# A fused group-norm and attention kernel: row maxima behind the projection in every unit 0 modulo 4, with shifts, gating and GpSimd's side work at other places

## The chip, the cores and the metric

The kernel runs on one core of a Trainium2 chip. The metric is the device time of one execution in microseconds (us); the median of three runs stands for a kernel.

## The reference, cut to what matters

```python
xn = silu(group_norm(x, gn_scale, gn_offset))          # x: (16, 32, 32, 512), 32 groups
q, k, v = split(einsum('bxyc,cd->bxyd', xn, w_qkv))    # 8 heads of 64
sim = einsum('bhdi,bhdj->bhij', q * 64 ** -0.5, k)     # 1024 x 1024 for each head
out = einsum('bhij,bhdj->bhid', softmax(sim), v)
return einsum('bxyd,dc->bxyc', out, w_out) + b_out + x
```

There are 16 images of 1024 tokens and 512 channels.

## The kernel before, in words

Every engine runs its own list of instructions, written out by hand, and meets the others at semaphores. An image is four **steps** of 16 **units**; a step is one pair of heads, and unit v = 16*s + u of an image is written (s, u) here. Images 2 to 14 repeat one pattern; a loop covers two images, and its back edge lies in front of (2, 0).

Numbers are carried as a high and a low float16 part. In unit v TensorE computes, in this order:

- **scores** of unit v (L1292, L1293): four matmuls of 512 columns into a slot of `ST`. `ST` has two slots, used in turn, so every user of a slot waits until the user before the last has been read (`wait_ring`).
- in even units the **maxima** of a later pair (L1192): four matmuls on 64 rows, into `TP` and into the next slot of `ST`. `maxima_place` says where they stand: 0 is directly behind the scores, 1 behind the product with V, 2 behind the projection. Before the change only the even unit behind a turned output block ((0, 4), (2, 4), (2, 12), (3, 8)) has 2, and u = 2 has 1.
- the **product with V** of unit v - 2 (L1322), into `PV`. The first of each four needs `pv_out`, that is, the sums of the four before have been taken out of `PV`.
- half of a **projection** into `SD` (L1177; a qk, v or out job lasts two units, part 0 in the even and part 1 in the odd one). Part 0 waits until the job before it has been drained (`side_drained`).
- in some odd units a **turn** (transposes): `xt` of the next image's input (L1250, at (0, 1), (0, 5), (0, 7), (0, 9)) or `ot` of an output (L1257, at (0, 3), (2, 3), (2, 11), (3, 7)). It stands in front of part 1 of the projection, or behind it where `turn_late` says so, which is only (0, 3) before.

ScalarE takes two exponentials of each slot, `P32` in float32 (L733) and `Ph` in float16 (L736), then its halves of the drains (L690, L695), the copies of turns (L705, L710) and the next image's `z` and `tanh` (L717, L724), at places in the tables `Z_AT` and `TANH_AT`.

VectorE makes the low probabilities `Pl` = P32 - Ph of one half of the columns (`low_probs`, L960) and GpSimd those of the other half (L615). VectorE's order in unit v is: the sums where v % 4 == 2 (L968 to L970), the drain of the job before (L848, L853, L860), `low_probs` of v - 1, the low part of a turned output (L881), a gating `z <- th, z` where `GATE_AT` says so (L946), then the two row maxima: `top_second` of the `ST` slot (L910; in the even unit, or in the odd one where maxima stand at place 2) and `top_use` of `TP` (L903, odd unit). After the fourth and the eighth block of rows (u = 9 and u = 1) a **shift** `ms <- mx` (L916) follows. SyncE's queue then copies the eight columns out and back as rows: `place_shift` waits for the shift, issues `shift_rows <- ms` (L456), waits for its landing, and issues two `QK <- shift_rows` (L460). Scores of u = 4 need those of u = 1's shift, scores of the next step's u = 0 those of u = 9's. SyncE's queue is in order: at (0, 1), `load_x` stands in front of `place_shift` and waits for the turn of that unit (`xt_filled`), since `x_in` is a single buffer.

GpSimd does in order, in each unit: `low_probs` of v - 1, `normalise` where v % 4 == 3 (L625), the statistics' small work ((1, 2), (1, 5)), `high_xn` (L598) in the unit of a gating and `low_xn` (L592) one unit later, and `add_bias` of the output blocks (L603) at `BIAS_AT` and `LATE_BIAS_AT`.

Of the kernel before, what the change touches and what calls it, by code (L numbers as in the profile page):

```python
# [10 lines left out]
ALU = mybir.AluOpType  # L11
# [119 lines left out]
def turn_late(step, u):  # L131

    return (step, u) == (0, 3)
# [7 lines left out]
def maxima_place(step, u):  # L141


    return 2 if output_turned(step, u) else 1 if u == 2 else 0
# [91 lines left out]
def conv_attention(nc, x, gamma, beta, w_qkv, w_out, b_out, out):  # L236
# [4 lines left out]
    with ctx:  # L241
# [26 lines left out]
        cns = sb("cns", [P, 4], F32)  # L268
# [98 lines left out]
        shift_ready = sem("shift_ready")  # L367
# [28 lines left out]
        def _(sp):  # L396
# [72 lines left out]
            def step(b, s, cnt, first=False, last=False):  # L469
                for u in range(16):  # L470
# [21 lines left out]
                    for pair, qb in unit_shift(s, u, last):  # L492
                        place_shift(b, pair, qb // 4)
# [40 lines left out]
        def _(pool):  # L534
# [95 lines left out]
            def step(b, s, par, first=False, last=False):  # L630
                for u in range(16):
# [48 lines left out]
        def _(act):  # L680
# [136 lines left out]
        def _(dve):  # L817
# [94 lines left out]
            def shift(qb, cnt):  # L912
# [4 lines left out]
                                        ALU.subtract, ALU.mult).then_inc(shift_ready, 1)  # L917
# [54 lines left out]

            def step(b, s, par, cnt, first=False, last=False):
                turned = []
                for u in range(16):
# [22 lines left out]
                    if u % 2 == output_turned(s, u - u % 2):  # L998
                        for use, slot in seconds:
                            top_second(use, cnt, slot)  # L1000
                    for use in unit_max(s, u - 1, last) if u > 0 else []:
                        top_use(use, b + 1, cnt)
                    for _, qb in unit_shift(s, u, last):
                        shift(qb, cnt)
# [458 lines left out]
```

## Time and profile before

| | before |
|---|---|
| median of 3 runs | 3598.46 us (3598.12 to 3598.59) |
| the profiled execution's own time | 3602.31 us |
| its span in the profile | 3600.6 us |
| TensorE matmuls busy | 3453.8 us (96%) |
| VectorE busy | 3047.2 us (85%) |
| ScalarE busy | 2698.3 us (75%) |
| GpSimd busy | 2020.2 us (56%) |
| granted TensorE clock | 0.994 of full speed |

A row of busy time by stretch has the bounds of the stretch and its length in us, then the busy us (and instructions) of TensorE's matmuls, its weight loads, VectorE, ScalarE and GpSimd, the granted TensorE clock as a share of full speed, the busy share of the DMA engines and GB/s. The stretches here begin and end at the first score matmul of a unit.

The span runs from the first to the last instruction. TensorE is nearly always busy, so the length of a unit, from one unit's first score matmul to the next unit's, is the natural measure: all 1024 of them together, with a prologue and an end, make the span. The ends of matmuls are modelled, so starts are the better number. A line of the timeline gives the start and the duration of an instruction (or of several merged ones), both in us, and in brackets how long the engine sat idle before it and for whom.

### The profile page before, as it was taken

To read this page: it belongs to the slowest core of one execution; us is meant where nothing else is said; L and a number is where in the kernel's file an instruction comes from. 1 tells how busy PE (TensorE), PEld (TensorE's weight loads), DVE (VectorE), ACT (ScalarE), POOL (GpSimd) and SP (SyncE) were. 2 spreads that over 40 slices of the span, in tenths; PEclk is the share of its full clock that TensorE was granted. 3 is DMA by queue.
4 is the path that set the end of the run, shared out by engine and by line. 5 is a ranking of instruction groups with operands and counts; after the bars stand their busy time and mean duration, and the time that the engine had idled before them with its cause. 6 is when DMAs were issued, how large, how long until landed. Compare 5 with 4: busy or idle time off the path is not lost. (4 is left out here: it accounts for less than half of the span.)

```text
span 3600.6 us, 89829 instructions
## 1 busy us (share of the span) xinstructions
PE 3453.8 (96%) x31822; PEld 1890.8 (53%) x31822; DVE 3047.2 (85%) x4011; ACT 2698.3 (75%) x2820; POOL 2020.2 (56%) x1998
## 2 busy tenths in 40 slices
PE   6899999999999999999999999999999999999998
PEld 2455555555555555555555555555555555555554
DVE  8788888888888887988888888888888888888887
ACT  3787777878778787787877778777777877877776
POOL 1464655646465474655646556465564656546556
PEclk8999999999999999999999999999999999999999
DMA  2213213222132322223133131321322213232231
GB/s 98 70 37 99 64 35 101 53 82 66 36 100 53 85 63 63 73 60 96 44 76 81 38 99 44 98 65 36 100 53 82 66 41 94 53 86 62 50 88 43
DMA packets 180060, 245.79 MB, mean 68 GB/s; under 512 B 51488, under 2 KB 84256, under 8 KB 179616
## 3 DMA queue, kind: packets, MB, share of 16 engines
q1 hardware_dynamic: 179616, 239.94, 25.6%
q8 instruction: 271, 4.44, 0.6%
q14 instruction: 173, 1.42, 0.1%
HBM read 88.35 MB, written 33.82 MB: 34 GB/s over the span
## 5 line engine op out<-in xcount | busy, mean ns | idle before, releaser
L615 POOL TENSOR_TENSOR Pl<-P,Ph 128x512 f16<-128x512 f32 x1024 | 1284.1, 1255 | 1402.0 <-ACT Ph L736 1394.5
L733 ACT ACTIVATE P<-ST,cns 128x1024 f32<-128x1024 f32 x1024 | 1140.5, 1114 | 818.2 <-PE ST L1293 782.7
L736 ACT ACTIVATE Ph<-ST,cns 128x1024 f16<-128x1024 f32 x1024 | 1133.1, 1107 | 0.3 <-issue 0.3
L960 DVE TENSOR_TENSOR Pl<-P,Ph 128x512 f16<-128x512 f32 x1024 | 1013.7, 990 | 72.8 <-ACT Ph L736 67.9
L1322 PEld LDWEIGHTS PV<-V,Ph 128*128 128x128 f16 x10240 | 760.5, 97 | 295.2 <-issue 127.2
L1322 PE MATMUL PV<-V,Ph 128*128 128x129 f16 (+2 forms) x10240 | 864.0, 210 | 37.8 <-DVE pv_sum L970 28.5
L1322 PE MATMUL PV<-V,Pl 128*128 128x65 f16 x8192 | 832.7, 192 | 1.9 <-issue 1.9
L1292 PE MATMUL ST<-QK 128*128 128x512 f16 x2048 | 777.9, 380 | 36.4 <-DMA QK<-shift_rows 22.2
L1293 PE MATMUL ST<-QK 128*128 128x512 f16 x2048 | 777.0, 379 | 0.0
L1322 PEld LDWEIGHTS PV<-V,Pl 128*128 128x128 f16 x8192 | 721.9, 98 | 66.4 <-issue 0.3
L1177 PE MATMUL SD<-X,wq 128*128 128x512 f16 x3036 | 741.9, 381 | 12.6 <-DVE wq L1067 9.2
L910 DVE TENSOR_REDUCE mx<-ST 128x1 f32<-128x1024 f32 x512 | 622.8, 1216 | 25.9 <-PE ST L1192 25.6
L903 DVE TENSOR_REDUCE mx<-TP 128x1 f32<-128x1024 f32 x512 | 620.7, 1212 | 0.0
L1177 PEld LDWEIGHTS SD<-X,wq 128*128 128x128 f16 x3036 | 278.8, 98 | 334.5 <-issue 28.0
L1177 PE MATMUL SD<-wq,X 128*128 128x512 f16 x1488 | 360.9, 379 | 4.3 <-DVE wq L1067 2.8
L1177 PE MATMUL SD<-wo,OT 128*128 128x512 f16 x1440 | 349.9, 379 | 1.6 <-DVE res L860 1.6
L1192 PE MATMUL TP<-QK 64*128 64x512 f16 x1024 | 317.0, 390 | 20.2 <-DVE mx L903 10.1
L1292 PEld LDWEIGHTS ST<-QK 128*128 128x128 f16 x2048 | 201.2, 98 | 248.5 <-ACT Ph L736 43.3
L848 DVE SCALAR_TENSOR_TENSOR QK<-SD,sc,QK 128x512 f16<-128x512 f32 x253 | 189.5, 749 | 153.7 <-ACT QK L690 133.6
L1192 PE MATMUL ST<-QK 64*128 64x512 f16 x1024 | 317.4, 390 | 0.0
L1293 PEld LDWEIGHTS ST<-QK 128*128 128x128 f16 x2048 | 199.8, 98 | 171.2 <-issue 1.1
L625 POOL TENSOR_TENSOR O<-pv_sum,den 128x256 f32<-128x256 f32 x256 | 224.1, 876 | 1.5 <-DVE pv_sum L970 1.5
(133 smaller groups left out, 2752.3 us busy)
## 6 DMA issues: line engine op xcount, KB each, us to landing
QK<-QK SPq DMA_DIRECT2D x384, 256.0 KB, 4.7
x_in<-in_x SPq DMA_DIRECT2D x61, 512.0 KB, 4.2
res<-in_x SPq DMA_DIRECT2D x120, 256.0 KB, 3.6
out<-res SPq DMA_DIRECT2D x120, 256.0 KB, 2.8
V<-V SPq DMA_DIRECT2D x16, 1040.0 KB, 6.9
QK<-shift_rows SPq DMA_DIRECT2D x256, 64.0 KB, 2.9
V<-in_L_conv_w_qkv SPq DMA_DIRECT2D x4, 768.0 KB, 9.8
shift_rows<-ms SPq DMA_DIRECT2D x128, 2.0 KB, 3.1
```

The lines of the kernel that those rows point to most:

```text
L615: nc.gpsimd.tensor_tensor(Pl[:, v % 4, HALF:], P32[:, v % 2, HALF:], Ph[:, v % 4, HALF:], ALU.subtract).then_inc(lo_pool, 1)
L625: nc.gpsimd.tensor_tensor(O32[:, pair % 2, 4 * q:4 * q + 4, rows_of(hh)], pv_sum[:, half % 2], den[:, half % 2, :].unsqueeze(2).to_broadca ...
L733: nc.scalar.activation(P32[:, v % 2, :], ST[:, slot, :], ACT.Exp, scale=cns[:, 0:1])
L736: nc.scalar.activation(Ph[:, v % 4, :], ST[:, slot, :], ACT.Exp, scale=cns[:, 0:1]).then_inc(exp_done, 1)
L903: nc.vector.reduce_max(mx[:, 0, qb:qb + 1], TP[:], AX.X).then_inc(top_drained, 1)
L910: nc.vector.reduce_max(mx[:, 1, qb:qb + 1], ST[:, slot], AX.X).then_inc(top_read, 1)
L960: nc.vector.tensor_tensor(Pl[:, v % 4, 0:HALF], P32[:, v % 2, 0:HALF], Ph[:, v % 4, 0:HALF], ALU.subtract).then_inc(lo_dve, 1)
L1177: ins = nc.tensor.matmul(bank, stationary(i, c), moving(j, c), start=(c == 0 and i + j == 0), stop=(c == CC - 1 and i == 1))
L1192: ins = nc.tensor.matmul(bank[:, bass.ts(kh, HALF)], QK[r, q_hi, block], QK[r, k_hi, bass.ts(kh, HALF)], start=True, stop=True)
L1292: nc.tensor.matmul(dst, QK1[:, at, 1, kb], QK1[:, at, 0, bass.ts(q, HALF)], start=True, stop=False)
L1293: ins = nc.tensor.matmul(dst, QK2[:, at, 1, kb], QK2[:, at, 0, bass.ts(q, HALF)], start=False, stop=True)
L1322: ins = nc.tensor.matmul(PV[:, cols], stationary, moving, start=kb == qb == n == 0, stop=kb == TB - 1, skip_group_check=True)
```

## The change

- Maxima stand at place 2, behind part 0 of the projection, in every unit 0 modulo 4; u = 2 keeps place 1 and the other even units place 0.
- Turns in units 1 modulo 4 ((0, 1), (0, 5), (0, 9)) stand behind part 1 of the projection.
- VectorE reads both maxima of a unit 0 modulo 4 in the unit behind it; in u = 1 it does so, with the shift, in front of `low_probs`.
- The shift of the first half moves from VectorE at u = 9 to ScalarE at u = 10 (an activation with a scale and a bias column), and its `place_shift` to u = 11. The one semaphore for shifts becomes two.
- `Z_AT`, `TANH_AT`, `GATE_AT`, `BIAS_AT` and `LATE_BIAS_AT` get other units.
- GpSimd waits for VectorE's `low_probs` of v - 1 before a low half or a bias.

```diff
 def turn_late(step, u):
-    return (step, u) == (0, 3)
+    return u % 4 == 1 or (step, u) == (0, 3)
...
 def maxima_place(step, u):
-    return 2 if output_turned(step, u) else 1 if u == 2 else 0
+    return 2 if u % 4 == 0 else 1 if u == 2 else 0
...
-Z_AT = [(1, 7), (1, 8), (1, 10), (1, 14), (2, 2), (2, 4), (2, 8), (2, 10)]
-TANH_AT = [(1, 8), (1, 10), (1, 12), (2, 0), (2, 4), (2, 6), (2, 8), (2, 12)]
-GATE_AT = [(1, 9), (1, 11), (1, 13), (2, 1), (2, 5), (2, 7), (2, 9), (2, 13)]
-BIAS_AT = {(3, 0): 0, (3, 2): 1, (3, 5): 2, (3, 6): 3}
-LATE_BIAS_AT = {(1, 0): 4, (1, 7): 5, (1, 8): 6, (1, 10): 7}
+Z_AT = [(1, 8), (1, 10), (1, 12), (1, 14), (2, 2), (2, 4), (2, 8), (2, 10)]
+TANH_AT = [(1, 9), (1, 11), (1, 12), (2, 0), (2, 2), (2, 6), (2, 8), (2, 10)]
+GATE_AT = [(1, 11), (1, 13), (1, 15), (2, 1), (2, 3), (2, 7), (2, 9), (2, 11)]
+BIAS_AT = {(3, 4): 0, (3, 6): 1, (3, 10): 2, (3, 12): 3}
+LATE_BIAS_AT = {(1, 0): 4, (1, 4): 5, (1, 8): 6, (1, 10): 7}
...
 # SyncE
                     for pair, qb in unit_shift(s, u, last):
-                        place_shift(b, pair, qb // 4)
+                        if qb == 7:
+                            place_shift(b, pair, 1)
+                    for pair, qb in unit_shift(s, u - 2, last):
+                        if qb == 3:
+                            place_shift(b, pair, 0)
...
 # GpSimd
+                    high, low = halves_at(s, u)
+                    if (low and not last) or ((s, u) in BIAS_AT and not last) or ((s, u) in LATE_BIAS_AT and not first):
+                        pool.wait_ge(lo_dve, UNITS * b + v)
...
 # ScalarE
+            def shift(tops):
+                blocks = slice(0, 4)
+                act.wait_ge(top_drained, tops)
+                nc.scalar.activation(ms[:, :, blocks], mx[:, :, blocks], ACT.Identity, scale=-1.0 / (HD * ROWC),
+                                     bias=cns[:, 4:5]).then_inc(shift_ready[0], 1)
...
                     exponentials(b, v, cnt)
+                    if u == 10 and unit_shift(s, u - 1, last):
+                        shift(cnt.top)
...
 # VectorE
+            def maxima(b, s, u, cnt, seconds, last):
+                if u % 2 == (maxima_place(s, u - u % 2) == 2):
+                    for use, slot in seconds:
+                        top_second(use, cnt, slot)
+                for use in unit_max(s, u - 1, last) if u > 0 else []:
+                    top_use(use, b + 1, cnt)
+                for _, qb in unit_shift(s, u, last):
+                    if qb == 7:
+                        shift(qb, cnt)
...
+                    if u == 1:
+                        maxima(b, s, u, cnt, seconds, last)
                     if not (first and v == 0):
                         low_probs(b, v - 1)
...
+                    if u != 1:
+                        maxima(b, s, u, cnt, seconds, last)
```

## Rows read from the trace of the kernel before

**Rows 1.** Busy time by stretch: thirteen images, a plain pair of units, other units
```profile
527.17:3389.75 2862.58, 2791.53 (x25850) 1531.12 (x25848) 2436.87 (x3185) 2186.99 (x2289) 1641.19 (x1638) 1.00 0.27 68
1664.38:1670.77 6.39, 6.39 (x66) 3.43 (x63) 6.13 (x11) 4.25 (x5) 2.92 (x3) 1.00 0.39 103
1641.79:1645.31 3.52, 3.52 (x38) 1.74 (x35) 2.79 (x4) 3.05 (x4) 0.94 (x2) 1.00 0.00 0
1638.05:1641.79 3.74, 3.74 (x37) 2.58 (x36) 2.37 (x3) 2.67 (x4) 2.19 (x3) 1.00 0.15 35
```

**Rows 2.** Waits over the whole run: engine, line, releaser, total us, times, longest
```profile
PE ST L1292 <- DMA QK<-shift_rows: 22.2, 28, 3.0
```

**Rows 3.** Busy time by stretch: unit (0, 5) of image 7
```profile
1645.31:1649.82 4.51, 3.97 (x38) 2.52 (x37) 2.65 (x3) 3.03 (x3) 2.56 (x2) 1.00 0.10 27
```

**Rows 4.** Busy time, then timelines of VectorE and TensorE: (1, 10), image 7
```profile
1716.36:1721.30 4.94, 3.65 (x37) 1.75 (x35) 4.90 (x7) 4.06 (x5) 4.91 (x5) 1.00 0.04 2
...
1714.81 1.51 DVE L946 SCALAR_TENSOR_TENSOR z<-th,z 128x512 f32<-128x512 f32 x1
1717.48 1.09 DVE L916 TENSOR_SCALAR ms<-mx,cns 128x8 f16<-128x8 f32 x1
...
1719.29 0.23 PE L1322 MATMUL PV<-V,Ph 128*128 128x129 f16 x1 [1.16 <-DVE pv_sum L970]
```

**Rows 5.** Busy time by stretch: (1, 8) and (1, 12), image 7
```profile
1709.75:1713.49 3.74, 3.72 (x37) 1.77 (x35) 2.11 (x3) 3.74 (x5) 3.74 (x4) 1.00 0.13 48
1724.17:1727.94 3.77, 3.58 (x37) 1.74 (x35) 3.77 (x5) 3.02 (x4) 3.67 (x3) 1.00 0.41 146
```

**Rows 6.** Busy time by stretch: (2, 2) with (2, 3), images 7 and 8
```profile
1743.60:1753.24 9.64, 7.59 (x74) 4.48 (x72) 6.96 (x11) 7.10 (x9) 5.52 (x6) 1.00 0.31 75
1965.34:1973.74 8.40, 7.59 (x74) 4.48 (x72) 6.88 (x11) 6.87 (x9) 5.29 (x6) 1.00 0.25 39
```

**Rows 7.** Busy time of (2, 5) with (2, 6), and VectorE's timeline there
```profile
1756.75:1763.70 6.95, 6.71 (x62) 3.51 (x61) 6.24 (x10) 6.51 (x8) 5.25 (x5) 1.00 0.70 174
...
1757.85 0.85 DVE L946 SCALAR_TENSOR_TENSOR z<-th,z 128x512 f32<-128x512 f32 x1 [0.71 <-ACT th L724]
1758.63 1.21 DVE L910 TENSOR_REDUCE mx<-ST 128x1 f32<-128x1024 f32 x1
```

**Rows 8.** Busy time by stretch: unit (3, 7) of image 7
```profile
1818.38:1822.32 3.94, 3.94 (x37) 2.51 (x36) 3.14 (x3) 2.62 (x3) 2.14 (x3) 1.00 0.01 4
```

**Rows 9.** Timelines of VectorE and GpSimd: low probabilities beside a bias, (1, 10)
```profile
1719.81 1.64 DVE L960 TENSOR_TENSOR Pl<-P,Ph 128x512 f16<-128x512 f32 x1
...
1719.62 1.29 POOL L603 TENSOR_TENSOR res<-res,bias 128x512 f32<-128x512 f32 x1
```

**Rows 10.** Timelines: a drain in (0, 0), VectorE's maxima in (0, 5), TensorE in (0, 4)
```profile
1627.91 0.75 DVE L848 SCALAR_TENSOR_TENSOR QK<-SD,sc,QK 128x512 f16<-128x512 f32 x1 [1.23 <-ACT QK L690]
...
1645.61 1.22 DVE L910 TENSOR_REDUCE mx<-ST 128x1 f32<-128x1024 f32 x1
...
1643.36 1.46 PE L1177 MATMUL SD<-wo,OT 128*128 128x512 f16 x6
1646.89 1.09 PE L1250 MATMUL ST<-ident,x_in 128*128 128x128 f32 x8 [0.54 <-DVE mx L910]
```

**Rows 11.** Timelines of TensorE and SyncE's queue in (0, 1) to (0, 3)
```profile
1631.37 1.04 PE L1250 MATMUL ST<-ident,x_in 128*128 128x128 f32 x8
1640.21 1.04 PE L1257 MATMUL ST<-ident,O 128*128 128x128 f32 x8
...
1632.58 0.38 SPq L414 DMA_DIRECT2D x_in<-in_x  x1
1633.11 0.37 SPq L456 DMA_DIRECT2D shift_rows<-ms  x1
1637.92 1.10 SPq L460 DMA_DIRECT2D QK<-shift_rows  x2
```

**Rows 12.** DMA issues of the page: count, KB each, median us to landing
```profile
QK<-shift_rows SPq DMA_DIRECT2D x256, 64.0 KB, 2.9
```

More of the change, by code:

```diff
@@ L267, in conv_attention @@
         tot = sb("tot", [P, 8], F32)
-        cns = sb("cns", [P, 4], F32)
+        cns = sb("cns", [P, 5], F32)
         absg = sb("absg", [P, CC], F32)
@@ L366, in conv_attention @@
         v_moved = sem("v_moved")
-        shift_ready = sem("shift_ready")
+        shift_ready = [sem(f"shift_ready{half}") for half in range(2)]
         shift_row = [sem(f"shift_row{half}") for half in range(2)]
@@ L452, in place_shift @@
             def place_shift(b, pair, half):
-                sp.wait_ge(shift_ready, 8 * b + 2 * pair + half + 1)
+                sp.wait_ge(shift_ready[half], 4 * b + pair + 1)
                 sp.dma_start(rows[half].rearrange("h (p j) -> p h j", j=4), ms[:, :, 4 * half:4 * half + 4]
@@ L641, in step @@
                         coefficients(b + 1)
+                    high, low = halves_at(s, u)
+                    if (low and not last) or ((s, u) in BIAS_AT and not last) or ((s, u) in LATE_BIAS_AT and not first):
+                        pool.wait_ge(lo_dve, UNITS * b + v)
                     if not last:
-                        high, low = halves_at(s, u)
                         for i in high:
@@ L916, in shift @@
                 nc.vector.tensor_scalar(ms[:, :, blocks], mx[:, :, blocks], cns[:, 3:4], -1.0 / (HD * ROWC),
-                                        ALU.subtract, ALU.mult).then_inc(shift_ready, 1)
+                                        ALU.subtract, ALU.mult).then_inc(shift_ready[qb // 4], 1)
             def guess(image, tops):
@@ L997, in step @@
                         seconds = [(use, cnt.next_slot()) for use in unit_max(s, u, last)]
[L998 to L1004, printed above, removed]
+                    if u != 1:
+                        maxima(b, s, u, cnt, seconds, last)
                     turned = [(use, cnt.next_slot()) for use in unit_turn(s, u, first, last)]
@@ L1105, in _ @@
             then(nc.vector.reciprocal(cns[:, 2:3], cns[:, 0:1]))
-            nc.vector.tensor_scalar(cns[:, 3:4], cns[:, 2:3], SHIFT_UP, None, ALU.mult).then_inc(setup_done, 1)
+            then(nc.vector.tensor_scalar(cns[:, 3:4], cns[:, 2:3], SHIFT_UP, None, ALU.mult))
+            nc.vector.tensor_scalar(cns[:, 4:5], cns[:, 3:4], 1.0 / (HD * ROWC), None, ALU.mult).then_inc(setup_done, 1)
             dve.wait_ge(setup_done, 1)
```

## The prediction

> **What bounds the kernel.** I first read busy time by stretch. Images 2 to 14 take 2862.58 us, 220.2 us each, TensorE is busy in 2791.5 us of it, and its clock is granted in full throughout [rows 1]. So TensorE's list sets the time, and the question is only where it stands still. I then took the units one by one. A plain pair (even with maxima, odd without) is 6.39 us, an even unit with its maxima at place 2 is 3.52 us, the same as with place 0 in that pair (6.39 less an odd unit of 2.87), and an odd unit with a turn is 3.74 us [rows 1], so a turn costs 0.88. An image without any wait is 32 x 6.39 + 8 x 0.88 + about 0.4 for the two statistics = 211.9 us. The whole prize is therefore some 8.3 us an image, 3.8%. The change removes no work from TensorE and adds none; it can only open or close such gaps. Last I read in which units the gaps lie and which instruction ended them. A unit longer than its plain length is a stall in it or in front of the next scores. All terms below are per image, and 15 images have them (the last has no next image to prepare, the first is nearly regular).
>
> **Gains.**
>
> 1. (0, 5) takes 4.51 us [rows 3] instead of 3.74. The turn starts at 1646.89 after 0.54 us idle, behind the read of the `ST` slot that began at 1645.61 and took 1.22 [rows 10]. Behind part 1 of the projection the turn comes 1.3 us later (1640.21 in a unit starting at 1638.05, against 1631.37 in one starting at 1630.51 [rows 1, 11]), when the read is over. Gain 0.77.
> 2. (1, 10) takes 4.94 us against 3.52: the product with V waited 1.16 us for the sums, which stood behind a gating of 1.51 us and a shift of 1.09 us [rows 4]. The gating leaves (1, 9) and this shift leaves VectorE. In its place both maxima are read in (1, 9), and the sums end about 1.5 us into (1, 10), as the product wants them. Gain 1.4.
> 3. (1, 8) and (1, 12) are 0.22 and 0.25 us too long [rows 5]: a bias behind the Newton steps, and a late read of `TP`. The bias moves to (1, 4), and there pushes the Newton steps, so that ScalarE's exponentials of unit 7 come later and the scores behind (1, 8) wait some 0.1. Gain 0.3.
> 4. (2, 2) with (2, 3) takes 9.64 us in image 7 and 8.40 in image 8, against 3.52 + 3.74 = 7.26 [rows 6]. In the first a shift is held on VectorE just as the 1.09 us one was [rows 4] and then arrives late. Afterwards it isn't held, since it runs before GpSimd has anything to do, but low probabilities and a gating now stand between the shift and the sums of (2, 2). These are two float32 passes of about 0.6 to 0.7 us; the sums end 1.73 us into (2, 2) and not 1.04, the product starts at 1.79, and the pair comes to 8.2 us. Gain between 0.2 and 1.4; I take 0.4, near image 8, because the DMA is waited for in only 28 steps of 64 [rows 2].
> 5. (2, 5) with (2, 6) takes 6.95 us against 6.39: with place 2 in the unit before, gating (1757.85, 0.85 us) and then the read of `ST` (1758.63, 1.21 us) end at 1759.84, and the scores of the next unit start at 1759.89 [rows 7]. (2, 13) with (2, 14) has the same pattern. Both gatings move to 3 modulo 4. Gain 2 x 0.57 = 1.15.
> 6. Turns at (3, 7) (3.94 us against 3.74 [rows 8]) and (2, 11) (half as much) wait for a read pushed by GpSimd's work, which now starts later. Gain 0.3.
> 7. In steps 1 and 3 the shift of u = 1 comes about 0.2 us earlier, because it no longer waits for low probabilities; where the scores of u = 4 wait for its rows that is gained. 0.15.
>
> Together 4.5 us.
>
> **Costs.**
>
> 8. Two gatings stay in, or come to, units 1 modulo 4 whose even unit now has place 2: (1, 13) and (2, 9). That is the pattern of term 5, so at least 0.57 each, 1.15. What is worse: `low_xn` now waits for low probabilities on VectorE that end 2.3 us or later into the unit, runs 1.2 us, and is still running when the exponentials end at about 3.2. Beside a GpSimd bias of 1.29 us, VectorE's low probabilities took 1.64 us and not about 0.7 [rows 9]: they wait until GpSimd's instruction is over. The gating behind them waits for GpSimd's own half in the same way. At (1, 13) this chain can bring 1.4 instead of 0.57, with ScalarE's `z` late as well. I take 1.7 for both; bounds 1.15 and 2.1.
> 9. Part 0 of the projection needs the drain before it. In (0, 0) the drain starts at 1627.91 and takes 0.75 [rows 10], ending 1.68 us into a unit that starts at 1626.98. With place 0 the projection started 2.2 us in and this was hidden by the maxima. With place 2 it starts 1.57 us in (1643.36 in the unit from 1641.79 [rows 1, 10]). A start follows what it waited for by 0.06 (reads end at 1646.83, the turn starts at 1646.89 [rows 10]), so 1.74: 0.17 of stall. It hits u = 0 of all four steps, (2, 8) and (3, 12), and some images at (3, 4): 6 x 0.17 and a bit; (2, 0) is worse if the late chain of term 8 reaches it. I take 1.2; bounds 0.9 and 1.6.
> 10. The late turn of (0, 1) holds SyncE's queue. Today the turn starts at 1631.37, `load_x` is issued at 1632.58 and only then, at 1633.11, the shift; the rows are back in the queue at 1637.92, and the two placing copies are issued in 1.10 us [rows 11]. They land a median of 2.9 us after issue [rows 12], so about 1641.4, and the scores of (0, 4) start at 1641.79 [rows 1]. The turn moves 1.3 us back and all of this with it, 1.3 less 0.4 of slack = 0.9 us in image 7, and the full 1.3 in images that wait for these rows already (the 22.2 us in 28 waits [rows 2]). I take 1.1; bounds 0.5 and 1.5. On this queue the reload of `x_in` moves too, for (0, 5)'s turn: it keeps some 0.3 us of slack for the turn of (0, 7).
> 11. (2, 4) and (2, 12): maxima at place 2 wait for a turned output's low part, which stands behind low probabilities that GpSimd may hold. 0 to 0.7; I take 0.2, because only one of the two chains reaches it.
>
> Together 4.2 us (3.0 at the least, 5.9 at the most; at the least of all 2.55 if (1, 13) and the drains are hidden by earlier waits).
>
> **Costed at nothing.** Place 2 itself (3.52 against 3.52 [rows 1]). The shift on ScalarE: it follows the exponentials of (s, 10), whose slot has idle time behind it, and its rows are wanted only six units later; uncovered it would be about 0.2 us each, 0.9 an image. Its `place_shift` at u = 11 blocks SyncE's stores for some 5 us, as it did at u = 9. The read of both maxima in one odd unit: low probabilities end 0.4 us in, the two reads at 1.5 and 2.7, in front of the next scores at 2.87. The biases of step 3 have a free GpSimd around them.
>
> **The sum.** -4.5 + 4.2 = -0.3 us an image, x 15 = -4 us. The profiled execution took 3602.3 us (span 3600.6), so it would take 3598; the median of the runs is 3.8 us lower, 3598.5, which gives 3594. About 0.2% (7.2 us) is what a measurement of this kernel can tell from no change; the forecast is inside it.
>
> **Rivals.**
>
> A. *The queues don't chain (faster).* GpSimd's later work never meets VectorE's low probabilities, term 8 stays near the plain pattern and terms 9 to 11 at the low end: 4.5 - 2.7 = 1.8 us an image, 27 us in full; with a part of it, 3576. For it: in step 3 of image 7 VectorE catches up within every four units. Against it: the drain of term 9 ends at a fixed 1.68 us, whatever the others do.
>
> B. *GpSimd's new wait becomes the bound (slower).* One mechanism: every low half and bias starts only when VectorE's low probabilities of the unit before are done. There are 16 of them in an image (8 low halves, 8 biases). Where it starts later than about 2 us into the unit, its 1.2 to 1.3 us run into the next low probabilities, as in [rows 9]. In a unit 0 modulo 4 the two maxima stand behind these, and their slack is 2.8 - 1.53 = 1.3 us: from a delay beyond that on, the next scores wait. If four places an image pay 0.35 more, that is +1.4, net +1.1 an image, +16 us: 3615. For it: units (1, 12) and (2, 8) have exactly this order. Against it: several of the even units carry no low half.
>
> C. *The shift's rows come in time (faster).* If the row copy of step 0 landed in 2.9 us, as the placing copies do at the median [rows 12], and not in the 4.4 us from 1633.48 to 1637.92 behind the load of `x_in` [rows 11], then issue ends 4.3 us into (0, 1), the rows are back at 7.2, placed copies are issued by 8.3 and landed at 11.2, and the scores of (0, 4) are due at 11.28. Term 10 falls away and today's wait of some 0.4 us in that step with it: 1.5 us an image, 3594 - 22 = 3572. Against it: the load stays directly in front. The Trainium skill, "DMA: Bandwidth & Descriptors", section "Anatomy of one DMA — SWDGE (gpsimd) path", gives a fixed cost of about 2.0 us per DMA plus bytes at 436 GB/s (for GpSimd's path), by which these small copies would be even earlier; this trace disagrees, with the 2.9 and the 4.4 us just named.
>
> D. *Nothing moves.* Stalls trade places and the sum is zero: 3598. TensorE's work is the same in both, so this is possible.
>
> **Chances.** The forecast 0.41 (3594, give or take 8: 0.14 of it is faster by over 0.2%, 0.25 within, 0.02 slower), A 0.22, B 0.25, C 0.05, D 0.07. Faster 0.14 + 0.22 + 0.05 = 0.41, same 0.25 + 0.07 = 0.32, slower 0.27. The range goes from the lower half of A, 3570, to B with a margin, 3616; the forecast's own is 3586 to 3602.
>
> **What would show it.** Step 1: (0, 5) at 3.74. Step 2: no gap in front of the product with V in (1, 10). Terms 4 and 5: (2, 2) still near 4.5, (2, 5) and (2, 6) at 2.87 and 3.52. Term 8: (1, 13) over 3.1 and (1, 14) over 3.8, scores starting right behind a read of `ST`. Term 9: the projection at u = 0 starting 1.74 us in. Term 10: `shift_rows` issued about 3.8 us into (0, 1), (0, 3) at 4.8 or more, and the waits for `QK<-shift_rows` well over 22.2 us in sum. The prediction is wrong on the fast side if drains are ready before 1.57 us or the rows land early, and on the slow side if low probabilities of u = 0 modulo 4 end over 1.3 us into the next unit.

## The result and the profile after

The changed kernel took 3607.55 us against 3601.46 us, medians of 20 runs each; the ratio is 1.0017, with a 95% interval of 1.001 to 1.0024. One of the changed kernel's 20 runs, at a granted clock of 0.75, took 4392.12 us; it is not in the ratio. The change makes the kernel slower by 6 us. The prediction had it 4 us faster. Both lie within the 0.2% that it called no change, on opposite sides. The profiled execution took 3612.2 us, its span 3610.4 us, 9.8 more than before. It lies 4.6 us above the median of its kernel, and the profiled one of before 0.9 us, so some 4 of these 9.8 us belong to these executions and not to the change.

First busy time by stretch in the changed kernel: images 2 to 14, then units of image 7: (0, 3), (0, 5), (1, 8), (1, 10), (1, 13), (1, 14), (2, 2) with (2, 3), (2, 5) with (2, 6), (3, 7). Columns as in [rows 1].

```profile
531.10:3397.44 2866.34, 2796.62 (x25849) 1539.01 (x25847) 2350.93 (x3133) 2201.30 (x2341) 1689.75 (x1638) 1.00 0.26 68
...
1639.07:1643.39 4.32, 3.91 (x37) 2.66 (x36) 2.89 (x4) 3.25 (x4) 2.76 (x3) 1.00 0.15 30
1646.91:1650.66 3.75, 3.75 (x39) 2.60 (x37) 2.66 (x3) 2.63 (x3) 1.88 (x2) 1.00 0.01 2
1712.67:1716.20 3.53, 3.53 (x37) 1.73 (x35) 1.04 (x3) 3.53 (x5) 2.91 (x4) 1.00 0.20 74
1719.08:1722.66 3.58, 3.58 (x37) 1.75 (x35) 3.58 (x7) 3.54 (x6) 1.89 (x2) 1.00 0.16 58
1729.13:1732.99 3.86, 3.04 (x30) 1.74 (x29) 3.86 (x4) 3.27 (x4) 3.16 (x3) 1.00 0.01 4
1732.99:1736.80 3.81, 3.67 (x33) 1.76 (x34) 3.81 (x7) 2.95 (x4) 1.89 (x2) 1.00 0.00 0
1746.33:1754.72 8.39, 7.42 (x73) 4.41 (x71) 8.35 (x11) 7.04 (x9) 6.60 (x6) 1.00 0.37 88
1758.50:1764.91 6.41, 6.41 (x63) 3.46 (x62) 5.70 (x10) 5.29 (x7) 2.57 (x3) 1.00 0.82 199
1819.69:1823.42 3.73, 3.73 (x37) 2.58 (x36) 1.80 (x2) 2.62 (x3) 2.73 (x4) 1.00 0.01 4
```

An image takes 2866.34 / 13 = 220.49 us instead of 220.20. The places where something was to be gained are at their plain length: (0, 5) 3.75 instead of 4.51 [rows 3], (1, 8) 3.53 instead of 3.74 [rows 5], (1, 10) 3.58 instead of 4.94 [rows 4], (2, 5) with (2, 6) 6.41 instead of 6.95 [rows 7], (3, 7) 3.73 instead of 3.94 [rows 8]. (1, 13), a plain odd unit of 2.87 before, takes 3.86, and TensorE is busy in only 3.04 of it. VectorE is busy in all 3.86.

The longer span is in images 2 to 14 (13 x 0.29 = 3.8), in the prologue (the first scores start at 93.55 us and not at 91.82), and in images 0, 1 and 15 with the end (1.8, 0.4 and 2.2). The prologue's part isn't shown to be an effect of the change: in the three experiments below on the kernel before, the first scores start at 92.20, 93.72 and 94.47 us.

The waits of the changed kernel, over the whole run, and of the costliest groups the two of low probabilities:

```profile
POOL X L597 <- DVE Pl L976: 109.2, 118, 3.6
...
PE ST L1318 <- DMA QK<-shift_rows: 25.7, 26, 3.5
...
PE ST L1318 <- DVE mx L926: 15.3, 31, 0.9
```

```profile
L620 POOL TENSOR_TENSOR Pl<-P,Ph 128x512 f16<-128x512 f32 x1024 | 1343.1, 1312 | 1179.3 <-ACT Ph L743 1172.2
...
L976 DVE TENSOR_TENSOR Pl<-P,Ph 128x512 f16<-128x512 f32 x1024 | 884.9, 864 | 206.7 <-ACT Ph L743 199.2
```

VectorE's low probabilities average 0.86 us instead of 0.99 (1013.7 us in 1024 before): GpSimd's side work does keep out of their way. The scores' wait for the rows of a shift rose from 22.2 [rows 2] to 25.7 us, and their wait for a read of `ST` is 15.3 us in 31 places: behind (1, 13), 0.8 us each, and behind (2, 9), 0.16 us each.

Here is every term of the prediction against the trace, in us per image: the mean over images 2 to 14 of a unit's length, after less before. What is not listed is within 0.05.

| term | predicted | measured |
|---|---|---|
| 1: (0, 5) | -0.77 | -0.76 |
| 2: (1, 10) | -1.4 | -1.34 |
| 3: (1, 8), (1, 12) | -0.3 | -0.31 - 0.18 = -0.49 |
| 4: (2, 2), (2, 3) | -0.4 | +0.11 - 0.27 = -0.16 |
| 5: (2, 5), (2, 6), (2, 13), (2, 14) | -1.15 | -0.27 - 0.42 - 0.28 - 0.29 = -1.26 |
| 6: (3, 7), (2, 11) | -0.3 | -0.23 - 0.12 = -0.35 |
| 7: (3, 3) | -0.15 | -0.19 |
| 8: (1, 13), (1, 14), (2, 9), (2, 10) | +1.7 | +0.95 + 0.28 + 0.31 + 0.26 = +1.80 |
| 9: u = 0 of four steps, (2, 8), (3, 12), (3, 4) | +1.2 | +0.76 + 0.42 + 0.19 + 0.06 = +1.43 |
| 10: (0, 3) | +1.1 | +0.63 |
| 11: (2, 4), (2, 12) | +0.2 | +0.25 + 0.24 = +0.49 |
| not foreseen: (0, 9), (0, 4), (3, 2) | 0 | +0.26 + 0.12 + 0.11 = +0.49 |

Gains 4.55, costs 4.84: together +0.29 where -0.3 was predicted. Two of the costs hold a single long unit each: (2, 8) is 0.18 too long in twelve images and 3.2 in image 14, and (0, 4) is 1.6 too long in one and regular in the rest.

The long (2, 8) is a loss of its own, once in an execution. The code from (2, 0) of image 14 on stands behind the loop. VectorE stands still there, and TensorE's projection waits for its drain:

```profile
3318.70 0.75 DVE L869 SCALAR_TENSOR_TENSOR V<-SD,sc,V 128x512 f16<-128x512 f32 x1 [3.26 <-issue]
...
3319.51 0.82 PE L1203 MATMUL SD<-wq,X 128*128 128x512 f16 x3 [3.06 <-DVE V L869]
```

"issue" says that VectorE waited for nothing that the profile shows; why it stood still is not known. The gap is there in all nine other traces of kernels with this change in them, and the unit is 6.6 to 8.4 us in all ten. In the kernel before and in the three kernels made from it VectorE has gaps of this kind at (2, 6) and (2, 8) of image 14 too (1.72 and 1.01 us in the kernel before), but the unit is 3.5 to 3.8 us. So 3.0 us here, and 4.7 in the second trace of the changed kernel, are lost once, in image 14, out of the 5 to 6 us by which the change makes the kernel slower. Without that unit the mean over the thirteen images is +0.06 and not +0.29.

### The profile page after: what moved, and what is told of

It reads as the page before. It is cut to its first block, busy times and chain, and to the rows that moved or that the text cites. A ratio compares the mean times of both kernels' runs of the same rounds, so it can differ in the third digit from the quotient of the medians.

```text
span 3610.4 us, 90056 instructions
## 1 busy us (share of the span) xinstructions
PE 3460.0 (96%) x31822; PEld 1902.0 (53%) x31822; DVE 2939.0 (81%) x3949; ACT 2715.7 (75%) x2883; POOL 2076.7 (58%) x1998
## 3 DMA queue, kind: packets, MB, share of 16 engines
q14 instruction: 177, 1.42, 0.2%
## 4 chain that ended last, share of the span: by engine, by line
PE 71%; DVE 8%; issue 7%; DMA 7%; ACT 3%; POOL 2%; SPq 2%; DVEq 0%; ACTq 0%; POOLq 0%
PE SD L1203 28%; PE PV L1348 15%; PE ST L1318 10%; PE ST L1319 9%; PE TP L1218 6%; DMA shift_rows<-ms 3%; DMA QK<-shift_rows 2%; DVE mx L919 1%; PE ST L1276 1%; DVE mx L926 1%; ACT Ph L743 1%; PE ST L1283 1%; POOL Pl L620 1%; DVE OT L897 1%; DMA x_in<-in_x 1%
## 5 line engine op out<-in xcount | busy, mean ns | idle before, releaser
L620 POOL TENSOR_TENSOR Pl<-P,Ph 128x512 f16<-128x512 f32 x1024 | 1343.1, 1312 | 1179.3 <-ACT Ph L743 1172.2
L976 DVE TENSOR_TENSOR Pl<-P,Ph 128x512 f16<-128x512 f32 x1024 | 884.9, 864 | 206.7 <-ACT Ph L743 199.2
L1318 PE MATMUL ST<-QK 128*128 128x512 f16 x2048 | 779.3, 380 | 55.6 <-DMA QK<-shift_rows 25.7
L630 POOL TENSOR_TENSOR O<-pv_sum,den 128x256 f32<-128x256 f32 x256 | 240.1, 938 | 1.5 <-DVE pv_sum L986 1.5
```

Of the source, the lines that this page charges most:

```text
L620: nc.gpsimd.tensor_tensor(Pl[:, v % 4, HALF:], P32[:, v % 2, HALF:], Ph[:, v % 4, HALF:], ALU.subtract).then_inc(lo_pool, 1)
L630: nc.gpsimd.tensor_tensor(O32[:, pair % 2, 4 * q:4 * q + 4, rows_of(hh)], pv_sum[:, half % 2], den[:, half % 2, :].unsqueeze(2).to_broadca ...
L976: nc.vector.tensor_tensor(Pl[:, v % 4, 0:HALF], P32[:, v % 2, 0:HALF], Ph[:, v % 4, 0:HALF], ALU.subtract).then_inc(lo_dve, 1)
L1318: nc.tensor.matmul(dst, QK1[:, at, 1, kb], QK1[:, at, 0, bass.ts(q, HALF)], start=True, stop=False)
```

## The experiments

The theory is that the two sums are real: each of the parts named opens or closes its own gap in TensorE's list, and the total is near zero by accident. Then undoing one part must move the units of its term and leave the others. The rivals are those of the prediction: that GpSimd's new wait is what costs (B), that the landing of the shift's rows and not the turn's place decides (0, 3) (C), and that nothing moves and stalls only trade places (D). The kernel before took 3617 to 3619 us on the four chips of the experiments and not 3598 to 3601 as in the first comparison (whose chip is called the first below); every ratio is to the kernel before on the same chip. No trace of the kernel before was taken on these chips. Units of the changed kernel's variants are compared with the changed kernel run again on one of the four; units that wait for a transfer differ between such traces by some tenths of a us whatever the edit ((0, 3) is 4.77 and 5.17 us in the two traces of the changed kernel, and 5.2 to 5.6 in the four variants that leave SyncE's queue as it is), so of these only the larger differences are read.

### The changed kernel again

> The changed kernel unaltered, on the same chip as the parts below, as their measure. Ratio 1.001 to 1.0025 as measured so far; if the waits for the shift's rows depend on the chip, (0, 3) and (3, 3) differ from 4.77 and 3.43 us and all other units don't.

3624.20 us against 3619.19, ratio 1.0016 (1.0007 to 1.0024). The result repeats. Against the trace of before, which is of the other chip, (0, 3) is 1.03 us longer here (0.63 in the first comparison), and `QK <- shift_rows` is waited for 35.4 us instead of 25.7. The units of terms 1 to 6 are within 0.03 of their changes on the first chip, (1, 13) is at +0.93; (0, 9) is at +0.10 and (3, 3) at +0.11. (2, 8) of image 14 takes 8.39 us. So what differs between the two traces are the units that wait for a transfer, (0, 3) above all, and that one unit. Two kernels made from the one before and run on this chip, described below, give a fairer measure of step 3 and of the pair (2, 2), (2, 3), which their edits don't touch: against them the pair is 0.37 and 0.43 shorter, and (3, 3) 0.16 and 0.19, where terms 4 and 7 said 0.4 and 0.15.

### GpSimd's wait taken out

```diff
-                    if (low and not last) or ((s, u) in BIAS_AT and not last) or ((s, u) in LATE_BIAS_AT and not first):
-                        pool.wait_ge(lo_dve, UNITS * b + v)
```

> The changed kernel without GpSimd's new wait for VectorE's low probabilities ahead of low halves and biases. Rival B of the prediction (this wait is the cost): 1.4 us an image come back, ratio about 0.996. Theory 1 (the wait only shifts one collision at (1, 13)): 0.4 us an image or less, ratio 0.9995 to 1.0015.

3628.85 us, ratio 1.0031 (1.0019 to 1.0043), where the theory said at most 1.0015 and rival B 0.996: not faster; the interval overlaps that of the changed kernel (1.0007 to 1.0024). By unit, (1, 13) becomes 0.50 shorter and (2, 9) 0.28 (the wait costs there as rival B said), but (2, 12) becomes 0.44 longer, (3, 7) 0.20 and (1, 6) 0.15; (0, 3) and (0, 9), which wait for transfers, 0.36 and 0.28. Busy time by stretch of this kernel in (1, 13) and (2, 12) of image 7, then its group of low probabilities on VectorE:

```profile
1743.06:1746.36 3.30, 3.04 (x31) 1.74 (x29) 3.30 (x4) 3.27 (x4) 2.60 (x2) 1.00 0.09 36
1795.28:1799.46 4.18, 3.58 (x37) 1.74 (x35) 3.94 (x4) 3.19 (x4) 2.73 (x3) 1.00 0.30 31
```

```profile
L974 DVE TENSOR_TENSOR Pl<-P,Ph 128x512 f16<-128x512 f32 x1024 | 1019.3, 998 | 178.9 <-ACT Ph L741 173.0 <-DVE mv L953 2.7 <-issue 0.4
```

(1, 13) is 3.30 and not 3.86; (2, 12) is 4.18 where the changed kernel has 3.77. Without the wait the mean is back at 1.00 us. So it is this wait that makes the low probabilities short. What it is worth in time is close to nothing: the units that don't wait for a transfer are 0.1 us an image shorter without it, in sum, and the rest of the difference, over 0.9 us, is in (0, 3), (0, 4), (0, 9), (1, 3) and (3, 3), which can differ without any edit. Rival B is refuted: its mechanism is there at two places, but the 1.4 us an image that it expected back don't come.

### Gatings out of the units behind place 2

```diff
-Z_AT = [(1, 8), (1, 10), (1, 12), (1, 14), (2, 2), (2, 4), (2, 8), (2, 10)]
-TANH_AT = [(1, 9), (1, 11), (1, 12), (2, 0), (2, 2), (2, 6), (2, 8), (2, 10)]
-GATE_AT = [(1, 11), (1, 13), (1, 15), (2, 1), (2, 3), (2, 7), (2, 9), (2, 11)]
+Z_AT = [(1, 8), (1, 10), (1, 12), (1, 14), (2, 2), (2, 4), (2, 6), (2, 10)]
+TANH_AT = [(1, 9), (1, 11), (1, 12), (2, 0), (2, 2), (2, 4), (2, 6), (2, 10)]
+GATE_AT = [(1, 10), (1, 12), (1, 15), (2, 1), (2, 3), (2, 7), (2, 8), (2, 11)]
```

> The changed kernel with the gatings of (1, 11), (1, 13) and (2, 9) moved to even units (1, 10), (1, 12) and (2, 8), and z or tanh of pieces 5 and 6 moved earlier to feed them. Theory 1: (1, 13), (1, 14), (2, 9), (2, 10) lose 0.95 + 0.28 + 0.31 + 0.26 = 1.8 us an image, some 0.3 may come back where the gatings land, ratio 0.994 to 0.996. Rival 2 (VectorE is simply full there, wherever the gating stands): the same 1.8 us turns up in (1, 10) to (1, 12) and (2, 8), ratio 1.001 or more.

3593.11 us, ratio 0.9931 (0.9918 to 0.9945), a little better than the 0.994 to 0.996 expected; against the changed kernel 0.9931 / 1.0016 = 0.9915. (1, 13) is 0.92 shorter, (2, 9) 0.38, (2, 10) 0.26, (2, 12) 0.23. (1, 10), (1, 12) and (2, 8), where the gatings went, don't grow (outside image 14, (2, 8) is 3.71 in both). Of term 8 only the 0.28 of (1, 14) stay. Unit (1, 13) of image 7, and VectorE's gatings of the whole run:

```profile
1728.07:1730.94 2.87, 2.87 (x30) 1.69 (x29) 2.80 (x3) 2.73 (x4) 2.87 (x3) 1.00 0.05 19
```

```profile
L962 DVE SCALAR_TENSOR_TENSOR z<-th,z 128x512 f32<-128x512 f32 x128 | 126.9, 992 | 0.1
```

This shows term 8. The gating is one of three things that the 0.95 us of (1, 13) needs: taking out GpSimd's wait gave back half of it, and with the maxima in their old places (below) it is gone too, gating and wait being where they were. Why it costs is seen in the changed kernel's timelines of VectorE, GpSimd and TensorE in (1, 13) of image 7, which starts at 1729.13:

```profile
1728.75 1.49 DVE L976 TENSOR_TENSOR Pl<-P,Ph 128x512 f16<-128x512 f32 x1 [0.29 <-ACT Ph L743]
1730.16 1.64 DVE L962 SCALAR_TENSOR_TENSOR z<-th,z 128x512 f32<-128x512 f32 x1
1731.72 1.21 DVE L926 TENSOR_REDUCE mx<-ST 128x1 f32<-128x1024 f32 x1
...
1728.53 1.16 POOL L597 TENSOR_TENSOR X<-z,X 128x512 f16<-128x512 f32 x1 [0.63 <-DVE Pl L976]
1729.64 1.61 POOL L620 TENSOR_TENSOR Pl<-P,Ph 128x512 f16<-128x512 f32 x1
...
1732.99 0.39 PE L1318 MATMUL ST<-QK 128*128 128x512 f16 x1 [0.82 <-DVE mx L926]
```

The low half ran 1728.53 to 1729.69 and VectorE's low probabilities end 0.55 us after it, at 1730.24; GpSimd's low probabilities then need 1.61 and not 1.16, and end at 1731.25; the gating ends 0.55 after those, at 1731.80. The read of `ST` can only then start, ends at 1732.93, and the scores start at 1732.99, 0.82 late. Two engines take turns, each held by the instruction of the other.

### The load of `x_in` behind the shift in SyncE's queue

```diff
 # SyncE, in the changed kernel and, alone, in the kernel before
-                        if u in (1, 5, 7):
+                        if u in (5, 7):
...
+                    if s == 0 and u == 1 and not last:
+                        load_x(b + 1, 1)
```

The second part stands behind the calls of `place_shift`.

> The changed kernel with one edit on SyncE's queue: at (0, 1) the load of x_in stands behind place_shift instead of in front of it, so the shift's rows no longer wait for the late turn. Theory 1 (each stall is a term of TensorE's list and they add up): rows issued 2.76 us into (0, 1) instead of 3.87, (0, 3) back to 3.74 us from a mean of 4.8, 1.0 us an image, ratio to the kernel before about 0.997 where the changed kernel has 1.0017. Rival (stalls trade places, or the DMA is simply late in step 0 for other reasons): (0, 3) stays over 4.4 or another unit takes the time, ratio 1.001 to 1.002.

> The kernel before with the load of x_in behind place_shift at (0, 1). Theory 1 (the rows of step 0 are late because the load stands in front of them, in the queue and on the DMA engines): (0, 3) falls to 3.74 us, 0.4 us an image or, where the chip's DMA is slower, up to 1.0, ratio 0.996 to 0.9985. Rival (the placing copies are slow whatever stands in front): ratio 0.999 to 1.001.

In the changed kernel: 3597.11 us, ratio 0.9941 (0.9928 to 0.9955), or 0.9925 of the changed kernel; 0.997 was expected. (0, 3) is 1.42 shorter, at its plain 3.74 in twelve images of thirteen, (0, 4) 0.12, and everything else is within 0.1. In the kernel before: 3607.84 us, 0.9972 (0.9962 to 0.9982), and (0, 3) is 3.74 too. SyncE's queue in step 0 of image 7, first in the changed kernel ((0, 1) starts at 1631.52), then in the kernel before with this one edit (1633.72):

```profile
1634.90 0.38 SPq L415 DMA_DIRECT2D x_in<-in_x  x1
1635.43 0.37 SPq L457 DMA_DIRECT2D shift_rows<-ms  x1
1639.53 0.46 SPq L461 DMA_DIRECT2D QK<-shift_rows  x1
```

```profile
1635.75 0.36 SPq L456 DMA_DIRECT2D shift_rows<-ms  x1
1638.93 1.11 SPq L460 DMA_DIRECT2D QK<-shift_rows  x2
1640.31 0.39 SPq L414 DMA_DIRECT2D x_in<-in_x  x1
```

The late turn puts the load at 3.4 us into the unit (2.1 before [rows 11]) and the shift's row copy at 3.9. The placing copies are issued when the rows have landed: 3.7 us after the end of the row copy's issue here and 4.4 in [rows 11], where the load stands in front; 2.8 us where it doesn't. The mean over images 2 to 14 says the same: 4.4 to 4.9 us in the nine traces with the load in front (3.6 at the least), 3.0 in the five with the load behind. So both the late issue and the slow landing of term 10 are shown. Rival C, that the rows land in 2.9 us with the load in front, is refuted; without it they do. In the changed kernel the edit gives 1.4 us an image.

### The late turns alone

```diff
 def turn_late(step, u):
-    return (step, u) == (0, 3)
+    return u % 4 == 1 or (step, u) == (0, 3)
```

> The kernel before with the late turns alone ((0, 1), (0, 5), (0, 9)). Theory 1: (0, 5) loses 0.77 us; at (0, 1) the load of x_in and the shift behind it in SyncE's queue come 1.3 us later, so (0, 3) gains 0.7 to 1.3, and the later load costs 0.1 to 0.3 in (0, 9): net 0 to +0.7 us an image, ratio 1.000 to 1.003. Rival (the late turn is free for the queue): only the 0.77 us, ratio 0.997.

In the kernel before: 3628.87 us, ratio 1.0032 (1.002 to 1.0043). (0, 5) is 0.76 shorter, as in the whole change, and (0, 3) 1.18 longer, against the first chip's trace of before. On the same chip, the kernel with place 2 alone (below) has the turn of (0, 1) in its old place and (0, 3) at 4.20 us, where this one has 5.32: 1.12 longer, the size of term 10. Moving these turns takes more at (0, 3) than it gives at (0, 5); in the changed kernel the edit of the queue above takes that away. (0, 9) is 3.84 here and 3.87 in the trace of before.

### Place 2 alone

```diff
 def maxima_place(step, u):
-    return 2 if output_turned(step, u) else 1 if u == 2 else 0
+    return 2 if u % 4 == 0 else 1 if u == 2 else 0
...
 # VectorE
-                    if u % 2 == output_turned(s, u - u % 2):
+                    if u % 2 == (maxima_place(s, u - u % 2) == 2):
```

> The kernel before with the headline alone: maxima behind the projection in every unit 0 modulo 4, and VectorE's reads in the odd unit behind it; turns, gatings, shifts and biases stay. Theory 1 (place 2 costs by itself and the other moves pay for it): six drains of 0.17 us, the turns at (0, 1) and (0, 9) wait for the read like (0, 5) does (0.77 each), gatings at (1, 9), (1, 13), (2, 1), (2, 9) give the 0.6 us pattern or worse, 3.5 to 5 us an image, ratio 1.015 to 1.021. Rival (place 2 gives VectorE's low probabilities room and pays for itself): ratio 0.995 to 1.003.

In the kernel before: 3697.70 us, ratio 1.0218 (1.0205 to 1.0232) where 1.015 to 1.021 was expected, 78.5 us or 5.2 us an image, more than the 4.2 that the prediction had for all costs together. By unit, per image, against the first chip's trace of before: (0, 1) +0.89, (0, 9) +0.72, (2, 10) +0.71, (1, 8) +0.65, (1, 9) +0.40, (1, 13) +0.33, (2, 2) +0.33, (1, 14) +0.28, (2, 3) +0.26, (2, 1) +0.24, u = 0 of three steps +0.58 together, (2, 8) and (3, 12) +0.19 each. Units (0, 1) and (1, 8) of image 7, and the turn in the first:

```profile
1671.56:1676.19 4.63, 3.96 (x39) 2.52 (x37) 2.93 (x4) 3.54 (x4) 2.60 (x2) 1.00 0.10 19
...
1752.62:1757.03 4.41, 3.69 (x38) 1.79 (x35) 2.38 (x3) 4.41 (x6) 4.41 (x5) 1.00 0.16 59
```

```profile
1673.26 1.09 PE L1250 MATMUL ST<-ident,x_in 128*128 128x128 f32 x8 [0.67 <-DVE mx L910]
```

The turn of (0, 1) waits for the read of `ST` just as that of (0, 5) did before [rows 10]. The whole change costs 0.17%, place 2 alone 2.2%: the other moves pay for it. At (0, 1) and (0, 9) it is the late turn that does; of the rest, which move pays how much was not tried one by one.

### Maxima at place 0 in u = 0, then everywhere as before

```diff
 def maxima_place(step, u):
-    return 2 if u % 4 == 0 else 1 if u == 2 else 0
+    return 2 if u % 4 == 0 and u > 0 else 1 if u == 2 else 0            # first
+    return 2 if output_turned(step, u) else 1 if u == 2 else 0          # second
```

> The changed kernel with the maxima of u = 0 back at place 0 (in front), those of u = 4, 8, 12 still behind the projection. Theory 1: the drain that ends 1.68 us into u = 0 is hidden again, units 0 of the four steps lose 0.17, 0.18, 0.16 and 0.25 us; both reads at u = 1 are over earlier, so the sums of (2, 2) end early and (2, 2) falls from 4.65 to about 3.8; (3, 3) waits less for its rows. About 2 us an image, ratio 0.993 to 0.995. Rival 2 (the reads in front of low_probs at u = 1 cost as much in whatever place the maxima stand): only the 0.76 us of the drains, ratio 0.9985.

> The changed kernel with every maximum where it stood before the change (place 2 only behind a turned output block); the late turns, the shift on ScalarE, gatings, biases, GpSimd's wait and VectorE's order at u = 1 stay. If place 2 is what costs (theory 1): beyond what the front place at u = 0 alone gave, the drains of (2, 8) and (3, 12) are hidden (0.4 us) and the gatings of (1, 13) and (2, 9) no longer hold up the scores (0.9 to 1.5 us), ratio 0.982 to 0.986. If place 2 away from u = 0 gives VectorE's low probabilities room that is worth something (rival): 0.989 to 0.993.

First kernel: 3583.16 us, ratio 0.9900 (0.9885 to 0.9915), 0.9884 of the changed kernel, where the theory had 0.993 to 0.995. (0, 0), (1, 0) and (3, 0) are 0.17, 0.17 and 0.24 shorter, which is term 9. More comes from elsewhere: (3, 3) is 0.86 shorter, (2, 2) 0.71, (1, 3) and (2, 4) 0.20 each, (3, 2) 0.11. With the `ST` maxima read in u = 0 only one read stands in front of the shift in u = 1, and the row copy of step 3 is issued 1.4 us earlier (its issue ends 1.70 us into (3, 1), not 3.14), so the scores of (3, 4) wait for nothing. Second kernel: 3553.38 us, ratio 0.9819 (0.9801 to 0.9836). Against the first, (1, 13) is 1.00 shorter, (2, 9) 0.36, (2, 10) 0.26 and (3, 12) 0.19, but (1, 8) 0.63 longer. So with everything else of the change in place, place 2 in its new units costs 1 - 0.9819 / 1.0016 = 2.0%.

### All of it together

> Three repairs of the changed kernel together: load of x_in behind place_shift at (0, 1), gatings at (1, 10), (1, 12), (2, 8), maxima of u = 0 in front. Theory 1 (stalls of one list add up): (0, 3) and (3, 3) at their plain 3.74 and 2.86 us, (1, 13) and (2, 9) at 2.87, ratio 0.975 to 0.980. Rival (they overlap, one hides the other): 0.984 or more.

> The same three repairs, and all other maxima back at their places of before too. Theory 1: the drains at (2, 8) and (3, 12) are hidden again, 0.4 us an image less than with the three repairs, ratio 0.973 to 0.979 and 0.001 to 0.002 below the three. Rival (with the gatings out of the way, place 2 at 4, 8 and 12 is the better place for VectorE): 0.001 or more above the three.

> The fastest so far (three repairs, maxima in front) with one unit's maxima put back behind the projection, those of (1, 8). There GpSimd's Newton steps make ScalarE's exponentials of unit 7 late, and maxima in front wait for them: (1, 8) is 4.16 us in that kernel and 3.54 in the changed one. Theory 1 (place 2 pays exactly where the exponentials are late): (1, 8) at 3.54, 0.6 us an image, ratio 0.970 to 0.9715. Rival (the wait only moves to the scores of (1, 9) or to (1, 10)): 0.9725 to 0.974.

| kernel (edits to the changed kernel) | us | ratio to before |
|---|---|---|
| queue, gatings, place 0 in u = 0 | 3529.86 | 0.9752 (0.9731 to 0.9773) |
| the same, maxima everywhere at the places of before | 3521.31 | 0.9730 (0.9714 to 0.9746) |
| the same, and place 2 at (1, 8) | 3515.50 | 0.9714 (0.9701 to 0.9727) |

The three edits multiply: 0.9925 x 0.9915 x 0.9884 = 0.9727 of the changed kernel, and 0.9752 / 1.0016 = 0.9736 was measured, so they are separate gaps, and the stalls don't trade places as rival D has it. In the second kernel of the table the largest regular gap left is at (1, 8), 4.16 us, where the maxima at place 0 wait 0.57 us for ScalarE's exponentials; place 2 there makes it 3.54. Images 2 to 14 of the last and fastest kernel:

```profile
515.94:3302.63 2786.69, 2772.32 (x25849) 1531.11 (x25847) 2302.44 (x3133) 2196.59 (x2341) 1672.11 (x1638) 1.00 0.28 70
```

214.4 us an image, where the prediction put an image without any wait at 211.9. So the late turns, the shift on ScalarE, the wait and the tables (with three gatings moved) gain 2.9% together with the better order of SyncE's queue, once place 2 is kept to where it is wanted. The shift on ScalarE was never tried by itself.

## Why the prediction was wrong

It was right in what moves. **Bound:** TensorE's list is the bound, and the change is worth what its gaps are worth; the larger effects show in unit lengths as they show in time. **Terms 1, 2, 5, 6, 7 and 8** came within 0.15 us of their sizes. The mechanism given is seen for 1, 2, 5 and 8: the turn behind part 1, the sums without a gating in front, scores right behind a read of `ST`. For term 6, (3, 7) is 0.20 longer again in the kernel without GpSimd's wait. For term 7 the row copy of step 3 is issued 3.14 us into (3, 1) and not 3.36, the 0.2 us that were forecast. Term 3 gave 0.49 for 0.3. Term 8's price was shown by the gatings' kernel. **Term 9** was worth its 1.2 (1.43 with the one long (2, 8)), with the projection starting as late as worked out. This is the changed kernel's drain and projection in (0, 0), which starts at 1627.82:

```profile
1628.75 0.75 DVE L864 SCALAR_TENSOR_TENSOR QK<-SD,sc,QK 128x512 f16<-128x512 f32 x1 [1.23 <-ACT QK L697]
...
1629.56 1.47 PE L1203 MATMUL SD<-X,wq 128*128 128x512 f16 x6
```

It starts 1.74 us in, the predicted number.

**The step that failed is "The sum": "-4.5 + 4.2 = -0.3 us an image, x 15".** It let a difference of 0.3 us carry the sign, where single terms were off by 0.1 to 0.5 us to both sides, and it took every loss for one that 15 images share. Measured is +0.29 over images 2 to 14, of which 0.23 is the stall in image 14, a thing for which the prediction had no term.

- The once-only losses. "x 15" took the first and last images for the others. The stall of VectorE in image 14 costs 3 to 5 us. Image 15 with the end is 2.2 us longer, image 0 1.8. Their cause was not tried; with the maxima of u = 0 in front, image 15 is back at 211.3 us (212.99 in the changed kernel, 210.82 before).
- Term 4, "I take 0.4": 0.16. In (2, 2) the gating is short (0.69 us), the sums end 1.75 us in, where 1.73 was said, and the product waits for them:

```profile
1746.72 0.69 DVE L962 SCALAR_TENSOR_TENSOR z<-th,z 128x512 f32<-128x512 f32 x1
1747.33 0.18 DVE L984 RECIPROCAL den<-PV 128x4 f32<-128x4 f32 x1
...
1747.53 0.55 DVE L986 TENSOR_REDUCE pv_sum<-PV 128x192 f32<-128x384 f32 x1
...
1748.32 0.22 PE L1348 MATMUL PV<-V,Ph 128*128 128x129 f16 x1 [0.97 <-DVE pv_sum L986]
```

  The product starts at 1.99 us, 0.24 behind the end of the sums and not 0.06, and the pair takes 8.39 instead of the 8.2 that I worked out. The 0.06 was read in [rows 10] behind reads of maxima; behind the sums the start follows by 0.06 to 0.28 us in the 28 places where the product waits for them, in the kernel before as in the changed one. On the other chip the gain is some 0.4 (above), with the pair at 8.44 us, since the kernels of before take longer there.
- Term 11, "I take 0.2, because only one of the two chains reaches it": both do, 0.25 and 0.24.
- Term 10, "I take 1.1": 0.63, and 0.75 with the one long (0, 4) behind it, inside its bounds. On another chip it is 1.0 to 1.1 (against the kernel with place 2 alone). This error alone would have made the kernel faster than forecast.
- The reload of `x_in`, "it keeps some 0.3 us of slack for the turn of (0, 7)": that turn is indeed not late. What the prediction left out is the next one. The late turn of (0, 5) delays the load for (0, 7); six copies `QK <- QK` stand behind that load in SyncE's queue and take 6.6 us to issue, and the load for (0, 9) stands behind them. In image 7 the last of the six ends 1.35 us behind the turn of (0, 7); in the kernel before they end just before that turn does. On average over the images the load is issued 2.9 us in front of (0, 9) instead of 3.8. (0, 9) is 0.26 an image longer, up to 1.9 us in a single one. That size isn't shown to be the change's: over the ten other traces with this late turn (0, 9) is 3.84 to 4.25 us, where the kernel before has 3.87, and the late turns alone gave 3.84. SyncE's queue and the turn that waits, image 7:

```profile
1650.30 0.38 SPq L415 DMA_DIRECT2D x_in<-in_x  x1
1650.78 4.25 SPq L448 DMA_DIRECT2D QK<-QK  x4
1655.08 2.36 SPq L451 DMA_DIRECT2D QK<-QK  x2
1657.61 0.47 SPq L437 DMA_DIRECT2D out<-res  x1
1658.35 0.46 SPq L415 DMA_DIRECT2D x_in<-in_x  x1
...
1665.48 1.06 PE L1276 MATMUL ST<-ident,x_in 128*128 128x128 f32 x8 [1.71 <-DMA x_in<-in_x]
```

  That the load is issued late is seen here; which of the transfers beside it makes it land 6.7 us after its issue was not tried.

Two slips in the numbers bear on nothing above: the least of the costs stands as 3.0, as 2.55 and, in rival A, as 2.7, where the lower bounds add to 2.55; and a turn costs 0.87, not 0.88.

**"Costed at nothing. Place 2 itself"** was right in the unit that it read (3.52), and is misleading as a statement on the change: alone it costs 2.2%, and in the changed kernel 2.0%. The prediction found these costs under other names (terms 8, 9 and 11) but missed the largest single one: at u = 0 it puts a second read in front of the shift, so (2, 2) and (3, 3) keep waits that would be gone (0.71 + 0.86). These don't show in a comparison of after with before, since before had them too. Of the other items there, the shift on ScalarE lengthened no unit. The read of both maxima in one unit did: in u = 1 it stands in front of the low probabilities, and most of (2, 4)'s 0.25 and all of (3, 2)'s 0.11 are gone in the kernel with the maxima of u = 0 in front.

**Rivals.** A fell on term 8. B has its mechanism at two units, and over the image next to nothing. C is refuted as put. D, that nothing moves, is refuted in its mechanism: gaps of 4.55 us closed and 4.84 opened. Its time, no change, is 6 us off, nearer than the forecast's. The forecast's 3594 would be 0.9988 of the kernel before; measured is 1.0017. That is inside the whole range, 3570 to 3616, and outside the forecast's own, 3586 to 3602. That the miss is small is luck in part: term 10 came out 0.5 us better than forecast, and the terms not foreseen 0.5 us worse.

## What to carry to other kernels

When the costs and gains of a reordering are each ten times their difference, the forecast is the list and not its sign: price the moves one by one, and run the ones that gain without the ones that pay for them. Look at the images one by one before multiplying: a stall that comes once, behind the loop, looked here like 0.23 us in every image. Ask of a move in one engine's list what queues behind it in a DMA queue that is served in order, since there an instruction that waits for a compute engine holds every small, urgent copy behind it. And a unit's length alone doesn't show a cost that was there before too: look also for the wait that should have gone and hasn't.

## What the runs showed of the hardware

VectorE and GpSimd, both on operands in SBUF, don't slow each other down evenly but alternate, an instruction at a time: in (1, 13) VectorE's low probabilities took 1.49 and its gating 1.64 us where 0.69 is the time undisturbed, each ending 0.55 us behind GpSimd's instruction, and GpSimd's own took 1.61 instead of 1.16. The same holds over the whole run: the 283 low probabilities and 105 gatings of the changed kernel that took over 0.9 us end 0.55 us behind a pass of GpSimd. VectorE's reads of PSUM were not held: 263 reads of maxima lie almost wholly beside GpSimd's passes, and none of the 1024 took over 1.23 us. The Trainium skill, "SBUF — State Buffer", section "Who interferes with whom", says that the two share one pair of ports, that this pair is an exclusive lock, and that a VectorE instruction with two SBUF inputs contends with a GpSimd instruction that reads SBUF; the trace agrees. Moving GpSimd's work away from the low probabilities (0.99 to 0.86 us on average) put it beside the gatings (1.01 us before, 1.33 after, 0.99 in the kernel with the gatings moved).

A copy of eight columns to rows took 3.0 us on average from the end of its issue to the next instruction of its queue, and 4.4 to 4.9 us directly behind the load of `x_in`. The same kernel before took 3598 to 3601 us in the first runs and 3617 to 3619 on the four chips of the experiments; of the changed kernel, the waits for `QK <- shift_rows` were 25.7 us in the first trace and 35.4 on one of the four, at the same granted clock (0.994 and 0.993). VectorE stood still for 3.0 to 3.3 us once, behind the end of the loop, in every kernel with the change in it; what it waited for, the profile doesn't show.
